# Attention on one core: exponentials turned by transposing DMAs, their low halves moved to GpSimd, query rotation in one instruction, all orders rewritten by group

## The reference, cut to what matters

```python
B, S, L = (2, 128, 128)
DIM_Q, H, K, D_C, D_CQ, R = (256, 16, 128, 64, 192, 64)
...
q_hk = (hidden_q @ Wq.T).reshape(Bv, Sv, H, K)
q_big = jnp.einsum('bshk,hkq->bshq', q_hk, w_kc_q)
...
q_big = _apply_rope(q_big, sin_q[None, :, None, :], cos_q[None, :, None, :])
...
q_r = jnp.einsum('bshq,hqr->bhsr', q_big, W_qr)
k_r = jnp.einsum('bld,hdr->bhlr', kv_r, W_kr)
scores = jnp.einsum('bhsr,bhlr->bhsl', q_r, k_r)
attn = jax.nn.softmax(scores, axis=-1)
ctx_c = jnp.einsum('bhsl,bld->bhsd', attn, kv_r)
ctx_lat = jnp.einsum('bhsd,hkd->bhsk', ctx_c, w_kc_kv)
ctx = ctx_lat.transpose(0, 2, 1, 3).reshape(Bv, Sv, H * K)
return ctx @ Wo.T
```

## Time and profile before

| What | Value |
|---|---|
| Median of 3 runs | 500.01 us (498.69 to 500.52) |
| Profiled execution, its own time | 502.39 us |
| Its span, first to last instruction | 500.6 us |
| Mean granted TensorE clock | 0.975 of full |
| Attention loop | some 143 to 363 us of the span |
| TensorE busy | 446.0 us, 89% |
| VectorE busy | 384.9 us, 77% |
| ScalarE busy | 283.3 us, 57% |
| GpSimd busy | 219.3 us, 44% |

### The profile page before, as it was taken

One profiled execution on the slowest core, in us unless ns is written; L12 is line 12 of the kernel. 1 busy time (PEld: TensorE's weight loads), 2 busy tenths in 40 slices (PEclk: granted clock), 3 DMA queues, 4 the chain that ended last, 5 costly groups with the idle time before them and its releaser, 6 DMA issues.

```text
span 500.6 us, 12052 instructions
## 1 busy us (share of the span) xinstructions
PE 446.0 (89%) x4688; PEld 343.2 (69%) x4688; DVE 384.9 (77%) x877; ACT 283.3 (57%) x628; POOL 219.3 (44%) x281
## 2 busy tenths in 40 slices
PE   3985898798899999999999989998789899999994
PEld 3445467357667778777777777776676688877773
DVE  4439998577668988886889788687577598888991
ACT  2667687775355655564565545565535266666660
POOL 3258141201423333333653445434633288888473
PEclk9997799999989999999999999999899999999998
DMA  8993004920450001000041000100101776777743
GB/s 263 267 341 76 0 2 128 364 83 1 120 176 2 1 10 77 2 3 1 1 107 67 2 1 1 46 22 8 36 10 46 212 204 195 178 199 217 195 46 34
DMA packets 38281, 46.89 MB, mean 94 GB/s; under 512 B 8016, under 2 KB 33616, under 8 KB 38032
## 3 DMA queue, kind: packets, MB, share of 16 engines
q1 hardware_dynamic: 33472, 40.95, 26.2%
q0 software_dynamic: 4224, 4.79, 5.6%
q10 hardware_dynamic: 528, 0.38, 0.3%
HBM read 40.27 MB, written 8.55 MB: 98 GB/s over the span
## 4 chain that ended last, share of the span: by engine, by line
PE 60%; DVE 18%; ACT 9%; issue 6%; POOL 3%; DMA 2%; SPq 1%; another core or an unknown queue 1%; POOLq 0%; ACTq 0%; DVEq 0%
PE psum L2055 9%; PE psum L1779 8%; PE psum L2071 7%; PE psum L1883 4%; DVE lw L1229 3%; PE psum L1846 2%; PE psum L1839 2%; PE psum L1704 2%; PE psum L1923 2%; PE psum L2076 2%; PE psum L1897 2%; DVE lw L1289 2%; PE psum L1864 2%; DVE nmax L1284 2%; DVE lw L1227 2%
## 5 line engine op out<-in xcount | busy, mean ns | idle before, releaser
L611 POOL TENSOR_TENSOR lw<-lw 128x512 f32<-128x512 f32 x48 | 60.8, 1270 | 109.2 <-DVE lw L1229 108.0
L1779 PE MATMUL psum<-lp 128*128 128x256 f16 x576 | 69.6, 276 | 2.1 <-DVE i L1342 2.1
L919 ACT ACTIVATE lw<-psum,nmax 128x256 f32<-128x256 f32 x128 | 59.4, 471 | 21.0 <-DVE nmax L1284 20.8
L926 ACT ACTIVATE lw<-psum 128x512 f16<-128x512 f32 x64 | 38.3, 598 | 43.8 <-PE psum L1883 43.8
L1779 PEld LDWEIGHTS psum<-lp 128*128 128x128 f16 x576 | 54.7, 99 | 9.4 <-DVE i L1342 2.4
L1289 DVE TENSOR_TENSOR lw<-psum,lw 128x512 f16<-128x512 f32 x64 | 43.6, 681 | 15.4 <-ACT lw L926 14.8
L2055 PE MATMUL psum<-lw,se 128*128 128x320 f16 x384 | 54.8, 299 | 0.2 <-ACT lw L995 0.2
L1005 ACT ACTIVATE lw<-psum,b1w 128x320 f16<-128x320 f32 x64 | 33.8, 528 | 37.0 <-PE psum L2055 36.7
L709 POOL DMA_INDIRECT out_x<-lw,tslot x24 | 44.5, 1856 | 17.4 <-DMA out_x<-lw,tslot 9.0
L1883 PE MATMUL psum<-identf,lw 128*128 128x128 f32 x256 | 41.7, 286 | 7.3 <-DVE lw L1289 5.1
L2055 PEld LDWEIGHTS psum<-lw,se 128*128 128x128 f16 x384 | 36.3, 97 | 16.8 <-DVE lw L1506 1.4
(11 more groups left out here) (246 smaller groups left out, 1021.1 us busy)
## 6 DMA issues: line engine op xcount, KB each, us to landing
se<-in_w SPq DMA_DIRECT2D x16, 1024.0 KB, 7.6
dispatch<-in_empty SPq DMA_DIRECT2D x4, 662.5 KB, 9.7
lp<-in_Wq SPq DMA_DIRECT2D x2, 1024.0 KB, 9.8
se<-in_WoT SPq DMA_DIRECT2D x1, 2048.0 KB, 11.7
lw<-dispatch SPq DMA_DIRECT2D x7, 265.0 KB, 7.4
lp<-in_w_kc_q SPq DMA_DIRECT2D x2, 768.0 KB, 10.0
x_sb<-in_x SPq DMA_DIRECT2D x2, 512.0 KB, 6.0
se<-in_gate_wT SPq DMA_DIRECT2D x1, 1024.0 KB, 8.9
```

The source lines that it names most:

```text
L611: nc.gpsimd.tensor_tensor(rope[:, c % QT, :], t1[:, c % 2, :], t2[:, c % 2, :], ALU.add)\
L919: A_(e_sb[:, n % 2, st * S:(st + 1) * S], bank[3 + n % 2][:, st * S:(st + 1) * S], ACT.Exp, bias=nmax[:, n % 2, st:st + 1], accum_out=esum ...
L926: A_(at[0][:, n % 2, :], turn_bank(n)[:, :], ACT.Copy).then_inc(a_at, 1)
L1779: ins = M(tile_bank(c)[:, half * S:(half + 1) * S], m1[w][:, kc, half, col:col + P], (yth, ytl)[a][:, kc, b * S:(b + 1) * S], start=(n == ...
```

## The change

- The exponentials are split before they are turned: `exps_high(n)` (ScalarE, SBUF to SBUF) and `exps_low(n)` (GpSimd; VectorE for the last two heads) write `hl[n % 2]`, 128 x 1024 in float16. SP issues a transposing DMA for it, `turned_exps(n)`, eight blocks of 128 x 128, into `turned[n % 3]`. `context(n)` waits for that DMA. `turn_scores`, `at_high`, `at_low` go.
- `exps(n)` waits for the low half of head n - 2, `exps_high(n)` for the DMA of head n - 2, the DMA of head n for the context of head n - 3.
- `turn(c)` is one instruction of 1024 columns, which reads the bank twice; sine and cosine are one table; `rotate(c)` reads the crossed product in swapped order.
- Every engine's loop runs by group. GpSimd's routing weights go to VectorE, routing of batches 0 to 2 uses bank 5, first expert's splits stand at heads 16 to 19, and the weights of experts 0 and 1 and the bias come in small pieces after each transposing DMA. In the tail VectorE and TensorE take `select` for two batches ahead of the last norm.

```diff
-SPLITS = (8, 12, 16, 32)
+SPLITS = (16, 17, 18, 19)
+PIECES = 16
...
+            def turned_exps(n):
+
+                if n < NHB - 2:
+                    sp.wait_ge(g_at, n + 1)
+                else:
+                    sp.wait_ge(v_at, n - NHB + 3)
+                if n >= 3:
+                    sp.wait_ge(p_cx, n - 2)
+                sp.dma_start_transpose(turned[n % 3].rearrange("p w st lt s -> p (w st lt) s"), hl[:, n % 2, :])\
+                    .then_inc(d_at[n % 2], 16)
...
+            for n in range(NHB):
+                turned_exps(n)
+                if n < PIECES:
+                    weight_piece(0, n)
+                elif PIECES + 6 <= n < 2 * PIECES + 6:
+                    weight_piece(1, n - PIECES - 6)
+                elif 2 * PIECES + 8 <= n < 2 * PIECES + 10 + NE:
+                    output_bias(n - 2 * PIECES - 8)
...
+            def exps_low(n):
+
+                if n < NHB - 2:
+                    pool.wait_ge(a_at, n + 1)
+                    nc.gpsimd.tensor_tensor(hl[:, n % 2, 512:1024], e_sb[:, n % 2, :], hl[:, n % 2, 0:512], ALU.subtract)\
+                        .then_inc(g_at, 1)
...
-                    act.wait_ge(p_at, n - 1)
+                    act.wait_ge(g_at, n - 1)
...
+            def exps_high(n):
+                act.wait_ge(a_exp, TPB * (n + 1))
                 if n >= 2:
-                    act.wait_ge(p_cx, n - 1)
-                A_(at[0][:, n % 2, :], turn_bank(n)[:, :], ACT.Copy).then_inc(a_at, 1)
+                    act.wait_ge(d_at[n % 2], 16 * (n // 2))
+                A_(hl[:, n % 2, 0:512], e_sb[:, n % 2, :], ACT.Copy).then_inc(a_at, 1)
...
+            for g in range(NGB):
+                n = g * G
+                exps(n + 1)
+                exps_high(n)
+                exps_high(n + 1)
+                route_steps(n)
+                exps(n + 2)
+                if g + 1 < NGB:
                     qz_high(g + 1)
+                route_steps(n + 1)
+                exps_high(n + 2)
+                exps(n + 3)
+                if g >= 1:
                     ct_high(g - 1)
+                route_steps(n + 2)
+                exps_high(n + 3)
+                if g + 1 < NGB:
+                    exps(n + 4)
+                route_steps(n + 3)
...
-                V.tensor_tensor(o[:, 0, :], r[:, 1, :], sn[:, 0, :], ALU.mult).then_inc(v_t2, 1)
-                V.tensor_tensor(o[:, 1, :], r[:, 0, :], sn[:, 1, :], ALU.mult).then_inc(v_t2, 1)
-                V.tensor_tensor(t1[:, c % 2, :], tile_bank(c)[:, :], cosq[:, c % QT, :], ALU.mult).then_inc(v_t1, 1)
+                V.tensor_tensor(t12[:, c % 2], tile_bank(c).unsqueeze(1).broadcast_to([P, 2, 2 * S]), rotq[:, c % QT],
+                                ALU.mult).then_inc(v_t1, 1)
...
-            def turn_scores(n):
...
-                pe.wait_ge(v_at, n + 1)
+                pe.wait_ge(d_at[n % 2], 16 * (n // 2 + 1))
...
+            for g in range(NGB):
+                n = g * G
+                scores(2 * g + 1)
+                if g >= 1:
+                    context(n - 2)
+                    context(n - 1)
+                route_steps(n)
+                if g + 1 < NGB:
+                    latent(g + 1)
+                if g + 2 < NGB:
+                    queries(QT * (g + 2))
+                context(n)
+                route_steps(n + 1)
+                if g + 2 < NGB:
+                    queries(QT * (g + 2) + 1)
+                if g >= 1:
+                    turn_context(g - 1)
+                route_steps(n + 2)
+                if g + 1 < NGB:
+                    scores(2 * g + 2)
+                if g + 2 < NGB:
+                    queries(QT * (g + 2) + 2)
+                context(n + 1)
+                if g >= 1:
+                    project(g - 1)
+                route_steps(n + 3)
```

More of the change, by code:

```diff
@@ L107, in program @@
         tabs = lp([2 * QT * 2 * S])
-        cosq, sinq = [tabs[:, i * 2 * QT * S:(i + 1) * 2 * QT * S].rearrange("p (a b) -> p a b", a=QT) for i in range(2)]
+        rotq = tabs.rearrange("p (c k s) -> p c k s", c=QT, k=2)
         kvT0 = lp([T])
@@ L154, in program @@
         e_sb = w2([2, 512])
-        at = [w2([2, 512], F16) for _ in range(2)]
+        turned = [w2([1024], F16) for _ in range(2)] + [y_sb[:, NT - TPB:NT, :].rearrange("p a b -> p (a b)").bitcast(F16)]
+        turned = [a.rearrange("p (w st lt s) -> p w st lt s", w=2, st=TPB, lt=TPB) for a in turned]
         cxn = w2([512])
@@ L610, in rotate @@
                     pool.wait_ge(p_qz, c // QT)
-                nc.gpsimd.tensor_tensor(rope[:, c % QT, :], t1[:, c % 2, :], t2[:, c % 2, :], ALU.add)\
-                    .then_inc(g_rope, 1)
+                straight, crossed = [t12[:, c % 2, k, :].rearrange("p (h s) -> p h s", h=2) for k in range(2)]
+                nc.gpsimd.tensor_tensor(rope[:, c % QT, :].rearrange("p (h s) -> p h s", h=2), straight, crossed[:, ::-1, :],
+                                        ALU.add).then_inc(g_rope, 1)
             def route_rows(b):
@@ L956, in route_normed, with route_steps @@
                     A_(y_sb[:, t, :], x_sb[:, t, :], ACT.Identity, bias=nb3[:, t:t + 1], scale=rstd[:, t:t + 1]).then_inc(s_y3, 1)
+            def route_steps(n):
+                for b in routed(n, 6):
+                    route_normed(b)
+                for b in routed(n, 9):
+                    route_turned(b)
+                for b in routed(n, 13):
+                    route_exp(b)
+                if n in SPLITS:
+                    split_high(SPLITS.index(n))
             qz_high(0)
@@ L1423, in _, with route_steps @@
             turn(5)
-            for n in range(NHB):
-                g, h = n // G, n % G
-                if n % 2 == 1 and n + 1 < NHB:
-                    maxima(n + 1)
-                if h == 0 and g >= 1:
-                    norm_sums(g - 1)
-                at_low(n)
-                if h == 0 and g >= 1:
-                    norm(g - 1)
-                if n % 2 == 1 and n + 2 < NHB:
-                    maxima(n + 2)
-                for c in tiles_at(n):
-                    turn(c)
-                if h == 1 and g + 1 < NGB:
-                    qz_low(g + 1)
-                if h == 2 and g >= 1:
-                    ct_low(g - 1)
+            def route_steps(n):
@@ L1441, in _ @@
                 for b in routed(n, 4):
                     update(b)
+                for b in routed(n, 5):
+                    route_stats(b)
+                for b in routed(n, 11):
+                    route_best(b)
+                    route_index(b)
+                for b in routed(n, 12):
+                    route_choice(b)
+                    route_sides(b)
+                for b in routed(n, 14):
+                    route_count(b)
+                    route_place(b)
+                    route_weights(b)
+                    route_meta(b)
@@ L1513, in _ @@
                     slot_meta(e + 1)
-                if e + 1 < NE:
-                    for q in range(0 if e >= 1 else 3, 4):
+                if e >= 1 and e + 1 < NE:
+                    for q in range(4):
                         split_low(4 * (e + 1) + q)
@@ L1910, in turn_context, with project @@
                 ins.then_inc(p_ct, 1)
-            def project(g, pairs=(0, 1)):
+            def project(g):
                 b = g // NG
@@ L1917, in project @@
                     pe.wait_ge(v_u2, b)
-                for pair in pairs:
+                for pair in range(2):
                     for a, w in PASSES:
```

299 lines of the change are left out of this document (122 added, 177 removed).

## The result

The changed kernel took 524.3 us in the median of four runs (517.0 to 526.5) against 499.4; the ratio leaves out the two runs of 526.3 and 526.5, which lie over 1.5% above the fastest, and is 1.0391 with an interval of 1.0315 to 1.0468. The forecast was 507 us, with 502.5 to 520 around it: the direction is right, on which the prediction had put no more than 0.50, and the size is not, since the loss is 20 to 25 us and not 7.

A forecast was written before the change was run, and what follows sets the result against it. Attention was taken as bound by TensorE, VectorE close behind. At L = 3.4, groups and routing gave +1.4 us, the last group +3.1, the start +2: +6.5, so 507 us; forecast 502.5 to 520, whole range 480 to 534.

The forecast's parts named there:

- L: Time from the end of a low half until its turned tile may be used; taken as 3.4 us, ends 1.8 and 5.9.
- Rival (b): A turned tile lands like a plain one, L 2.9 to 3.1: 497.5 to 502 us, no change; chance 0.12.
- the rivals at the two ends: L at or below 2.8: 494 or 480 us, chance 0.38; L = 5: 534, or blocks in series: 690, chance 0.14.
- (d): Tiles wait behind 128 KB weight pieces in the first 38 heads: 0.5 us for half, +4 us, inside the forecast's range.
- (c): Transposes bound by the DMA side: L = 5, 534 us; blocks in series, L = 14.4, 690 us; chance 0.14.
- The loop, L + 8.8: From one group's first low half to the next's, through DMA, context, query tile and rotations: 12.2 us a group.
- TensorE's floor: TensorE's work left in a group of four heads once the transposes go: 11.6 us, met by the loop at L = 2.8.
- Routing: Routing batches 0 to 2 inside the loop: 3.8, 0.5 and 8.0 us in a batch's three groups, 28.9 us in all.
- The last group, +3.1: Last norm-to-norm distance: two pairs of heads each need halves and DMA, 11.6 against 9.5 us, plus one for routing steps.
- The start, +2: At the start of attention the first low half stands behind the sixth rotation on GpSimd: +2 us.
- The rotation, at no gain: VectorE's query tile in one instruction of 1024 columns instead of three: put at 1.2 us, no gain.
- The step in the third group: Sign: a clear step of 6 to 8 us in a batch's third group, with GpSimd's indirect DMAs in it.

The follow-up runs named there:

- e11: The changed kernel unaltered, measured again in the round of e8 and e10: 523.1 us, 1.0500 of the kernel before.
- e6: The changed kernel with the high half turned by its own four-block DMA as soon as made: 527.3 us, 1.0608 of the kernel before.
- e3: The changed kernel with batches 0 and 1's scatters in pairs behind the second low half of groups 8, 10, 12, 14: 514.6 us, 1.0274.
- e7: The changed kernel with VectorE's routing steps behind the maxima and third rotation, in the last group behind the last low halves: 517.1 us, 1.0323.
- e8: The changed kernel with the moves of e3 and e7 together: 497.8 us, 1.0017 of the kernel before.
- e10: The changed kernel with small unused matmuls filling TensorE's longest waits: 521.9 us, 1.0456 of the kernel before.
- e5: The changed kernel with every transposing DMA of the first 62 heads issued twice: 561.4 us, 1.1261 of the kernel before.
- e16: e8 with every transposing DMA of the first 62 heads issued twice: 541.9 us, 1.0918 of the kernel before, 9.0% over e8.
- e2: The changed kernel with the four splits at heads 10, 14, 18, 22, still ahead of VectorE's maxima: 516.7 us, 1.0384 of the kernel before.
- e12: e8 with the splits at heads 10, 14, 18, 22, VectorE's piece behind the maxima: 500.5 us, 1.0049 of the kernel before.
- e13: e12 with the last two contexts ahead of the first gathering matmuls: 500.1 us, 1.0063 of the kernel before.
- e1: The kernel before with only the one-instruction rotation added, its old loop untouched: 496.3 us, 0.9936 of the kernel before.

## Why the prediction was right in kind and wrong in size

**L: right.** 3.2 us in the median, 3.4 taken. Rival (b), 2.9 to 3.1, is close by, and its 497.5 to 502 us did not come; the rivals at the two ends (2.8 and below; 5; blocks in series) are out. L was meant from the end of the low half, and there is more in it than the median of the landings: the second head of a pair can find SP busy for up to 2 us more, and in e11 the tiles of the 32 heads with a weight piece behind them land after 3.45 us on average, the 22 with nothing behind them after 3.21, about what (d) had put (0.5 us for half of them). Eight blocks land after 3.2 us and four after 2.5 (e6), so a DMA's blocks are not paid one behind another at 1.8 us each, as the far end of (c) had it. A turned tile lands a little later than a plain one: the output's plain 256 KB after 2.4 us here (2.9 before), the turned 256 KB after 3.2.

**The loop, L + 8.8: right for a plain group.** 12.2 forecast, 11.9 and 12.2 measured; in e11 13.1 and 13.5, an execution with the same order, so one profile is good to about 1 us a group. With e3, e7, e8 and e10, whose first two groups are the same, it is 11.6 to 13.5 and 12.4 on average. But the sum took it for thirteen groups, and the trace has two that are plain. The low half took 1.18, not 1.27; the high half, read from SBUF, took 0.63, where the copy from PSUM had taken the 0.60 that the sum kept as the most. The loop and TensorE's floor (11.2 to 11.4 of work, 11.6 forecast) nearly coincide. e5 and e16 bear out that the DMA is in the loop, without giving its share.

**Routing: near in size, wrong in kind.** 12.3 us a batch were forecast on top of four groups of 12.2, 8.0 of them in the third group; 14.3 and 13.1 came (63.1 and 61.9 less 48.8). They are spread: 14.9, 15.4, 14.8 and 18.0 in the first batch, 13.3, 16.3, 16.3 and 16.0 in the second. That the totals agree is in part luck. I had summed GpSimd's scatter and VectorE's steps as a price of the work. e8 does the same work and pays 5.1 and 4.3. Two thirds of it was a price of two places in two queues.

**The splits, not in the sum: this step failed.** The prediction put the weights' pieces at nothing ("nothing, but for what they add to L") and had no term at all for the first expert's splits, which the change moves together into heads 16 to 19, on two engines of the loop. The stretch that should have taken 48.8 took 53.8, +5.0, all of it in its last two distances, 15.0 and 14.7 (batch 0's update, 0.74 us of VectorE, is in the second). Before, a split stood in a group of 13.6 where the others had 13.5. In the changed kernel ScalarE's part takes 1.05 us as ever; VectorE's waits 3.5 us for the first of them with the maxima behind it, and takes 1.23 to 2.13 us instead of 1.22, while GpSimd's operations beside it grow too (the rotation from 1.27 to 2.24):

```profile
190.81 1.34 DVE L1339 SCALAR_TENSOR_TENSOR se<-se 128x1024 f16<-128x1024 f32 x1 [3.50 <-ACT se L949]
...
199.27 2.13 DVE L1339 SCALAR_TENSOR_TENSOR se<-se 128x1024 f16<-128x1024 f32 x1
...
200.28 2.24 POOL L641 TENSOR_TENSOR lw<-lw 128x512 f32<-128x512 f32 x1
```

The last section shows smaller VectorE operations stretched beside GpSimd's (0.76 to 1.07 us where four columns take 0.16). In e2 spreading the splits leaves the stretch as long, and in e12 putting them behind the maxima as well wins nothing over e8, which speaks for the work itself, as the rival to e12 said; how much of the 5.0 is theirs no run measured alone.

**The last group, +3.1: this step failed.** It was 18.1 and in e11 15.4, against 9.5: +8.6 and +5.9. The sum had the halves and their DMAs decide it. It lacked the 16 gathering matmuls that stand ahead of the last contexts in TensorE's queue, 4.43 us from 371.75; the first of the two last tiles is issued at 370.70 and is there by 373.9. Here it is, and below it the same 16 matmuls in e7:

```profile
371.75 4.43 PE L2033 MATMUL psum<-lw,se 128*128 128x320 f16 x16 [1.48 <-DVE lw L1430]
375.97 0.85 PE L1913 MATMUL psum<-lp,y_sb 128*128 128x64 f16 x12
```

```profile
372.37 2.33 PE L2034 MATMUL psum<-lw,se 128*128 128x320 f16 x16 [1.50 <-DVE lw L1430]
```

The context starts at 375.97, 2 us after its tile is there. Counted from norm 15, the 16 matmuls begin at 12.4 us in this profile, at 10.4 in e11 and at 10.2 in e7 and e8, and norm 16 starts 0.9 to 1.3 us after their end in all four. Two things set their end. One is the DMA of head 60: it landed after 4.8 us in this profile and after 3.1 to 3.2 in the other three, and ScalarE's high half waited 3.7 us for it against 2.0 in e11. The other is TensorE's clock. While the 16 run, the granted clock is 0.50 here and in e8 (4.43 us) and 1.00 in e7 (2.33 us). e7 and e8 have the same order in this group and the same start, and their distances are 13.6 and 15.6: that is the clock's price. TensorE idles 1.5 us just before the 16 in both, so what decides between the two levels no run shows. e10's added matmuls stood behind the gathering, so they did not test this. VectorE's routing steps hold the last two low halves for 2.7 us (the sum had one). With the 16 at the full clock and these steps ahead (e2) the distance is 15.2, with the steps behind (e7) 13.6, so both orders count. With the matmuls behind the contexts (e13) it is 13.5, and a microsecond of it comes back later.

**The start, +2: wrong in sign in one profile**, -3.1, and +1.3 in e11. The two executions of one order differ by 4.4 us there, more than the term.

**The rotation, at no gain: wrong.** e1 shows 3 us of gain. The 1.51 us of three instructions became 1.21; I had set the new instruction against itself. Whether the changed kernel keeps that gain no run shows.

**The account.** For the first profile: splits +5.0, routing +2.8, norm 13 to 15 -0.4, last group +5.5, start -5.1, end +0.2: +8.0 on top of 6.5, the 14.6 us by which the profiled executions differ (517.0 and 502.4). The remaining 10 us to the medians' difference of 24.9 are spread: this profile is the fastest execution of the changed kernel and the profile of before lies 2.4 us over its median. e11's profile, at 524.2, shows the typical case: +1.3 at the start, +14.0 in fourteen groups, +5.9 in the last. Against the forecast it has 8.1 more from norm 1 to 5: 5.9 in the two distances with the splits and 2.2 in the two plain groups, which are these:

```profile
158.21:171.31 13.10, 12.65 (x152) 9.39 (x156) 8.15 (x11) 6.96 (x22) 8.28 (x7) 0.89 0.65 120
171.31:184.81 13.50, 11.42 (x152) 8.64 (x152) 8.16 (x12) 7.35 (x23) 8.25 (x8) 1.00 0.70 118
```

In the first, the granted clock is 0.89 and TensorE is busy for 12.65 us instead of 11.24. The second has the full clock and is as long. ScalarE's waits in the two, one each, say why:

```profile
161.65 0.60 ACT L918 ACTIVATE lw<-psum 128x512 f16<-128x512 f32 x1 [2.65 <-PE psum L1878]
...
176.45 0.63 ACT L935 ACTIVATE lw<-lw 128x512 f16<-128x512 f32 x1 [2.50 <-DMA y_sb<-lw]
```

In the first it waits 2.65 us for the latent queries (1.08 in the second group of the first profile), whose matmuls last 0.63 us each at a granted clock of 0.50 (158.03 to 160.50) instead of 0.38 at 1.00, and the next high half stands behind it. So the clock cost about a microsecond here, where others wait for TensorE's work, other than in the waits that e10 filled. In the second, one transposing DMA, issued at 171.36, lands after 5.0 us instead of 3.1, and both the high half and the context wait for it. Why that one was late no run shows.

**What would show it**, point by point: the high half's wait of over a microsecond (1.2) came. The step in the third group (6 us over a plain one) came in batch 0; in batch 1 the group before is as long. TensorE's busy time fell by 23, not 40; at 0.45 a head the transposes alone were 29, and the mean clock fell from 0.975 to 0.949; at a lower clock matmuls last longer (the 16 gathering ones 4.43 us at 0.50, 2.33 at 1.00). GpSimd's rose by 58, not 80: 62 halves came to 72 us, not 79, and the routing weights went to VectorE, which I had left out.

## What to carry to other kernels

Cost a moved step by what stands behind it in each queue, not by its own duration: two places in two queues were worth 19 to 25 us here, and moving one of them alone gave 1 to 2%, since the other hole stayed or grew. A list of everything that a change moves, read off the order of every engine and not off the diff's headline, would have shown the splits. And an asynchronous link in a loop (here 3.2 us) makes the queues that feed it critical, even of engines that are idle half the time (GpSimd at 54% here).
